# A graph transformer on one core: TensorE's semaphore increments moved from the last product of a group to a drain behind it

## The reference

```python
for l in range(2):
    xn  = layernorm(x)
    xp  = xn + xn @ Wpos + bpos + deg * Wdeg + bdeg      # deg: standardized out-degree
    q, k, v = xp @ Wq + bq, xp @ Wk + bk, xp @ Wv + bv   # 8 heads of 16
    att = clip(sum(q[dst] * k[src]) / 4, -50, 50)
    alpha = softmax of att over the edges of each dst
    x   = x + segment_sum(v[src] * alpha, dst) @ Wo + bo
    x   = x + gelu(layernorm(x) @ W1 + b1) @ W2 + b2     # 128 -> 512 -> 128
out = layernorm(x_in + x)
```

## Time and profile before

| | us |
|---|---|
| median of 3 runs | 3657.33 |
| lowest, highest | 3653.97, 3659.31 |
| span of the profiled execution | 5559.9 |
| TensorE busy in it | 3461.6 (62%) |
| VectorE busy | 2916.7 (52%) |
| GpSimd busy | 2472.4 (44%) |
| ScalarE busy | 1771.1 (32%) |

### The profile page before, as it was taken

How to read it: one execution, slowest core, us unless ns; L and a number is a source line. 1 busy time by engine, 2 the same in 40 slices (tenths; PEclk the granted TensorE clock), 3 DMA queues, 4 the chain that set the end, 5 groups by cost and what they waited for, 6 DMA issues and landing times.

```text
span 5559.9 us, 72300 instructions
## 1 busy us (share of the span) xinstructions
PE 3461.6 (62%) x24196; PEld 2666.6 (48%) x24475; DVE 2916.7 (52%) x6780; ACT 1771.1 (32%) x4391; POOL 2472.4 (44%) x2597
## 2 busy tenths in 40 slices
PE   5834656655665656666566376666666566666666
PEld 4623445444454445444444254455555455545545
DVE  9944545554454545555455354554554454545455
ACT  2301232323333332323234133333333333333334
POOL 1065444444444444444542544445444454444443
PEclk7756777777777777777777677777777777777777
DMA  2133333333333333333332333333333333333332
GB/s 73 49 111 87 88 106 93 102 88 95 102 94 99 94 102 89 104 95 96 107 105 65 106 103 109 108 107 113 96 108 106 108 110 113 111 102 115 109 104 73
DMA packets 404556, 548.28 MB, mean 99 GB/s; under 512 B 78348, under 2 KB 318656, under 8 KB 403988
## 3 DMA queue, kind: packets, MB, share of 16 engines
q0 software_dynamic: 123648, 337.81, 20.9%
q1 hardware_dynamic: 273030, 198.56, 11.9%
q10 hardware_dynamic: 7506, 7.20, 0.4%
HBM read 518.00 MB, written 25.29 MB: 98 GB/s over the span
## 4 chain that ended last, share of the span: by engine, by line
PE 32%; another core or an unknown queue 30%; DVE 14%; issue 12%; ACT 10%; DVEq 0%; SPq 0%; DMA 0%; ACTq 0%
PE psum L952 7%; PE psum L993 4%; PE psum L1009 3%; ACT scratch L1227 3%; PE psum L1042 3%; PE psum L1026 3%; DVE att L1685 2%; PE psum L970 2%; ACT arena L1238 2%; DVE scratch L1676 2%; DVE kv_ring L1394 1%; PE psum L1123 1%; DVE work L1377 1%; DVE scratch L1700 1%
## 5 line engine op out<-in xcount | busy, mean ns | idle before, releaser
L1971 POOL DMA_INDIRECT kv_ring<-kv_table,src_idx x1936 | 1846.4, 954 | 2132.8 <-DVE scratch L1700 1501.1
L1227 ACT ACTIVATE scratch<-psum 128x512 f32<-128x512 f32 x1148 | 649.5, 570 | 2061.3 <-remote 1442.0
L952 PE MATMUL psum<-arena 128*128 128x256 f32 x1764 | 631.5, 486 | 464.2 <-issue 194.2
L1971 POOL DMA_INDIRECT arena<-kv_table,src_idx x640 | 607.8, 950 | 664.6 <-DVE scratch L1700 489.7
L1726 DVE SCALAR_TENSOR_TENSOR arena<-psum,in_block,arena 128x136 f32 x644 | 200.9, 353 | 1286.4 <-remote 1187.3
L993 PE MATMUL psum<-q_win,scratch 64*128 64x128 f32 x5152 | 534.3, 349 | 285.7 <-issue 149.9
L952 PEld LDWEIGHTS psum<-arena 128*128 128x128 f32 x1764 | 372.6, 236 | 621.0 <-issue 319.2
L1009 PE MATMUL psum<-scratch 128*64 128x136 f32 x5152 | 519.1, 330 | 185.4 <-issue 154.2
L993 PEld LDWEIGHTS psum<-q_win,scratch 64*128 64x128 f32 x5152 | 443.2, 243 | 343.1 <-issue 332.5
L1238 ACT COPY arena<-psum 128x512 f32<-128x512 f32 x504 | 265.1, 532 | 986.9 <-remote 524.7
L1685 DVE TENSOR_REDUCE att<-scratch 128x64 f32<-128x1024 f32 (+1 forms) x448 | 525.1, 1172 | 0.1
(11 more groups left out here) (251 smaller groups left out, 4873.9 us busy)
## 6 DMA issues: line engine op xcount, KB each, us to landing
arena<-kv_table SPq DMA_DIRECT2D x126, 896.0 KB
kv_ring<-kv_table,src_idx POOLq DMA_INDIRECT x1936
q_win<-q_table SPq DMA_DIRECT2D x644, 32.0 KB
work<-kv_table SPq DMA_DIRECT2D x98, 128.0 KB
arena<-kv_table,src_idx POOLq DMA_INDIRECT x640
q_win<-q_table SPq DMA_DIRECT2D x126, 64.0 KB
work<-q_table SPq DMA_DIRECT2D x98, 64.0 KB
kv_table<-work SPq DMA_DIRECT2D x49, 128.0 KB
```

Source lines behind the costliest of these rows:

```text
L952: mm = e.matmul(to[:, t % 2 * 2 * D:(t % 2 + 1) * 2 * D], hot_source[:, t * P:(t + 1) * P], source_rows[:, t, :], start=True, stop=True)
L1227: e.activation(to[:, at:at + width], apart[k % 2][:, 0:width], ACT.Relu, bias=1.0, scale=-1.0).then_inc(apart_read, 1)
L1971: e.indirect_dma_start(kv[m % RING_KV][:, t, :], None, kv_table[l], bass.IndirectOffsetOnAxis(ap=src_idx[:, c * T + t:c * T + t + 1], axis ...
```

## The change

In all groups of products of the edge and node stages and of the sorts, the increment is taken off the last matmul, and a drain of TensorE's queue, put behind the group, carries it. In `spread_chunk` one drain increments `spread` by 2. A `sum` of a block has its drain after the second half only. In `node_tensor` one drain stands at the end for all names. The products, their order and the waits stay as they are, as do the first stage and the other engines' programs.

```diff
 source_by_edge:
-            e.matmul(to[:, 0:len(ts) * P], place_source, ..., start=True, stop=True
-                     ).then_inc(apart_made, 1)
+            e.matmul(to[:, 0:len(ts) * P], place_source, ..., start=True, stop=True)
+            e.drain().then_inc(apart_made, 1)
 gather_rows, place_by_edge, edge_by_place: the same, one drain each
 spread_chunk:
-                    m = e.matmul(q_edge[h][:, t * P:(t + 1) * P], ...)
-                    if t == T // 2 - 1:
-                        m.then_inc(spread, 1)
+                    e.matmul(q_edge[h][:, t * P:(t + 1) * P], ...)
+            e.drain().then_inc(spread, 2)
 sum_chunk:
-            m.then_inc(edge_summed, 1)
+            e.drain().then_inc(edge_summed, 1)
 spread_queries:
-            m.then_inc(spread, 1)
+            e.drain().then_inc(spread, 1)
 sum_edges:
             if h == 1:
-                m.then_inc(edge_summed, 1)
+                e.drain().then_inc(edge_summed, 1)
 sort_tensor: in each of totals, slots and rank
-                mm.then_inc(sort_step, 1)
+                e.drain().then_inc(sort_step, 1)
 node_tensor: .then_inc(done, 1) taken off the last product of every name, and at the end
+            e.drain().then_inc(done, 1)
```

More of the change, by code:

```diff
@@ L939, in source_by_edge @@
             to = fill_bank(e, fill(n, "source", h))
-            e.matmul(to[:, 0:len(ts) * P], place_source, edges[:, ts[0] * P:(ts[-1] + 1) * P], start=True, stop=True
-                     ).then_inc(apart_made, 1)
+            e.matmul(to[:, 0:len(ts) * P], place_source, edges[:, ts[0] * P:(ts[-1] + 1) * P], start=True, stop=True)
+            e.drain().then_inc(apart_made, 1)
         def gather_rows(e, n, i):
@@ L951, in gather_rows @@
             for t in range(2 * i, min(2 * i + 2, TB)):
-                mm = e.matmul(to[:, t % 2 * 2 * D:(t % 2 + 1) * 2 * D], hot_source[:, t * P:(t + 1) * P], source_rows[:, t, :],
-                              start=True, stop=True)
-            mm.then_inc(apart_made, 1)
+                e.matmul(to[:, t % 2 * 2 * D:(t % 2 + 1) * 2 * D], hot_source[:, t * P:(t + 1) * P], source_rows[:, t, :],
+                         start=True, stop=True)
+            e.drain().then_inc(apart_made, 1)
         def place_by_edge(e, n, h):
@@ L961, in place_by_edge @@
             to = fill_bank(e, fill(n, "turn", h))
-            e.matmul(to[:, 0:width], of, edges[:, at:at + width], start=True, stop=True).then_inc(apart_made, 1)
+            e.matmul(to[:, 0:width], of, edges[:, at:at + width], start=True, stop=True)
+            e.drain().then_inc(apart_made, 1)
         def edge_by_place(e, n, h):
@@ L969, in edge_by_place @@
             for t in range(0, width, P):
-                m = e.matmul(to[:, t:t + P], edges[:, at + t:at + t + P], of, start=True, stop=True)
-            m.then_inc(apart_made, 1)
+                e.matmul(to[:, t:t + P], edges[:, at + t:at + t + P], of, start=True, stop=True)
+            e.drain().then_inc(apart_made, 1)
         def tensor_fill(e, l, what, u, h):
@@ L1025, in spread_queries @@
             for t in ts:
-                m = e.matmul(q_edge[f % 2][:, (t - ts[0]) * P:(t - ts[0] + 1) * P], hotT[n % 2][:, t * P:(t + 1) * P],
-                             q_win[:, n % 2, :], start=True, stop=True)
-            m.then_inc(spread, 1)
+                e.matmul(q_edge[f % 2][:, (t - ts[0]) * P:(t - ts[0] + 1) * P], hotT[n % 2][:, t * P:(t + 1) * P],
+                         q_win[:, n % 2, :], start=True, stop=True)
+            e.drain().then_inc(spread, 1)
         def sum_edges(e, l, u, h):
@@ L1041, in sum_edges @@
             for t in part_tiles(l, u, h):
-                m = e.matmul(edge_sum(l, u), hot[n % 2][:, t, :], msg[n % 2][:, t, :], start=t == 0, stop=t == last)
+                e.matmul(edge_sum(l, u), hot[n % 2][:, t, :], msg[n % 2][:, t, :], start=t == 0, stop=t == last)
             if h == 1:
-                m.then_inc(edge_summed, 1)
+                e.drain().then_inc(edge_summed, 1)
         def sort_tensor(e, s, k):
@@ L1056, in sort_tensor @@
                 for t in range(ST):
[L1057 to L1059 removed]
+                    e.matmul(ps[0:ST, 0:NT], one_tile[:, ST - 1 - t:2 * ST - 1 - t], s_oh[:, t // RUNS, :, t % RUNS],
+                             start=t == 0, stop=t == ST - 1)
+                e.drain().then_inc(sort_step, 1)
             elif name.startswith("slots"):
@@ L1062, in sort_tensor @@
                 for t in range(RUNS):
-                    mm = e.matmul(ps[0:2 * NT, 0:P], s_vals[:, :, :, t].rearrange("p v b -> p (v b)"), s_slot[:, :, t],
-                                  start=t == 0, stop=t == RUNS - 1)
-                mm.then_inc(sort_placed, 1)
+                    e.matmul(ps[0:2 * NT, 0:P], s_vals[:, :, :, t].rearrange("p v b -> p (v b)"), s_slot[:, :, t],
+                             start=t == 0, stop=t == RUNS - 1)
+                e.drain().then_inc(sort_placed, 1)
             else:
@@ L1070, in sort_tensor @@
                 e.matmul(flat, before[:], s_oh[:, q].rearrange("p b g -> p (b g)"), start=True, stop=False)
-                e.matmul(flat, ones_b[0:ST, :], s_carry[q % 2][0:ST].rearrange("p b g -> p (b g)"), start=False, stop=True
-                         ).then_inc(sort_ranked, 1)
+                e.matmul(flat, ones_b[0:ST, :], s_carry[q % 2][0:ST].rearrange("p b g -> p (b g)"), start=False, stop=True)
+                e.drain().then_inc(sort_ranked, 1)
         def node_tensor(e, l, j, k, held):
@@ L1090, in node_tensor @@
                 if held and j >= LAYERS[l].jb:
-                    mm = e.matmul(ps[:, 0:MW], ident[:], acc_b[:, LAYERS[l].place(j) % HELD_B, :], start=False, stop=True)
+                    e.matmul(ps[:, 0:MW], ident[:], acc_b[:, LAYERS[l].place(j) % HELD_B, :], start=False, stop=True)
                 elif held:
@@ L1095, in node_tensor @@
                         e.matmul(lower, fold[:], acc[:, row, :], start=False, stop=row == ring_rows(2 * j)[-1])
-                    mm = e.matmul(upper, fold[:], acc[:, (2 * j + 1) % RING_W, :], start=False, stop=True)
+                    e.matmul(upper, fold[:], acc[:, (2 * j + 1) % RING_W, :], start=False, stop=True)
                 else:
@@ L1101, in node_tensor @@
                         e.matmul(upper, ident[:, 0:HALF], acc_all[:, 2 * j + 1, :], start=False, stop=False)
-                    mm = e.matmul(ps[:, 0:MW], ident[:], acc_all[:, 2 * j, :], start=False, stop=True)
-                mm.then_inc(done, 1)
+                    e.matmul(ps[:, 0:MW], ident[:], acc_all[:, 2 * j, :], start=False, stop=True)
             elif name == "sums_t":
                 e.wait_ge(mean_ready, nth(l, j, ""))
-                e.transpose(ps[:, 0:P], row, ident[:]).then_inc(done, 1)
+                e.transpose(ps[:, 0:P], row, ident[:])
             elif name == "out_proj":
@@ L1109, in node_tensor @@
                 e.matmul(ps[:, 0:D], ones_b[0:3, :], row_parts[:, l, 0, :], start=True, stop=False)
-                e.matmul(ps[:, 0:D], col, w_o[:, l, :], start=False, stop=True).then_inc(done, 1)
+                e.matmul(ps[:, 0:D], col, w_o[:, l, :], start=False, stop=True)
             elif name == "hidden_t":
                 e.wait_ge(norm_row, norms(l, j, 0))
-                e.transpose(ps[:, 0:P], row, ident[:]).then_inc(done, 1)
+                e.transpose(ps[:, 0:P], row, ident[:])
             elif name == "ff_in":
@@ L1116, in node_tensor @@
                 for i in range(FC):
-                    mm = e.matmul(ps[:, i * P:(i + 1) * P], w_1[:, l, i * P:(i + 1) * P], col, start=True, stop=True)
-                mm.then_inc(done, 1)
+                    e.matmul(ps[:, i * P:(i + 1) * P], w_1[:, l, i * P:(i + 1) * P], col, start=True, stop=True)
             elif name == "ff_out":
@@ L1122, in node_tensor @@
                 for i in range(FC):
-                    mm = e.matmul(ps[:, 0:D], g[:, i * P:(i + 1) * P], w_2[:, l, i, :], start=False, stop=i == FC - 1)
-                mm.then_inc(done, 1)
+                    e.matmul(ps[:, 0:D], g[:, i * P:(i + 1) * P], w_2[:, l, i, :], start=False, stop=i == FC - 1)
             elif name == "next_t":
                 e.wait_ge(norm_row, norms(l, j, 1))
-                e.transpose(ps[:, 0:P], row, ident[:]).then_inc(done, 1)
+                e.transpose(ps[:, 0:P], row, ident[:])
             elif name == "qkv":
                 e.wait_ge(next_ready, i + 1)
-                e.matmul(ps[:, 0:QKV], col, w_qkv[:, l + 1, :], start=True, stop=True).then_inc(done, 1)
+                e.matmul(ps[:, 0:QKV], col, w_qkv[:, l + 1, :], start=True, stop=True)
+            e.drain().then_inc(done, 1)
         def tensor_edges(e):
```

8 lines of the change are left out of this document (4 added, 4 removed).

## The result

The changed kernel takes 4382.27 us (median of 4 runs, 4379.76 to 4383.57), the kernel before 3657.29: ratio 1.199 [1.1973, 1.2007], 725 us slower. Forecast were 4040 us and a range of 3700 to 4500. The direction and the place held; the size was nearly twice the forecast.

A forecast was written before the change was run, and what follows sets the result against it. GpSimd's gathers were taken to bound the kernel at 3657 us; drains would make TensorE the bound, exceeding the gathers by 212 us in layer 0 and 171 in layer 1: 3657 + 212 + 171 = 4040 us, range 3700 to 4500.

The forecast's parts named there:

- The pace before: GpSimd's indirect gathers, 1.25 us apart, set the pace; their sum of 3633.6 us is 0.6% under the median.
- What a drain does: On TensorE's full queue: lost tail overlap (0.16 or 0.07 us), exposed first weight load (0.10 or half), and gap g.
- would have left 3950: If mode switches already drain TensorE, 1288 full/half-array boundaries lose no 0.07 us overlap: 90 us less than 4040.
- TensorE becomes the bound, the ring fills: Main case, 0.78: TensorE exceeds the gathers by 212 and 171 us, the four-chunk ring fills, gathers wait; likeliest 4040 us.
- The increments' lateness is nothing: Increments reach ScalarE and VectorE some 0.1 us later: nothing behind the slot's cover, under 5 us at the layers' ends.
- I take g = 0.12: Gap from products' end to next dispatch behind a drain, two 0.06 us handoffs, range 0 to 0.28; sign: far from 0.12.
- I charge nothing for 1.2: TensorE's clock: the drained queue is as busy, so no time is added for running at 1.2 GHz.
- The products' own time: TensorE's work at full clock without gaps, 1478 and 1481 us in the two layers' counted stretches, partly estimated.
- That is the cover: 400 us per layer: TensorE's undrained 1226 and 1167 us against 1650 and 1570 us of gathers leave 400 us per layer, which drains use up.
- Hidden: Rival, 0.08: the drain passes on dispatch or g is under 0.03, TensorE stays under the gathers; 3657 us, within 5.
- faster: Rival, 0.04: increments on matmuls come slightly late in unrecorded runs too, a drain's do not; at most 24 us gained, 3634.
- All of it counts: Rival, 0.10: TensorE was the bound already, so 354 + 363 us of tails and loads and 444 of gaps add: 4818.

The follow-up runs named there:

- second profile: The kernel before, unchanged, profiled once more: 3644.22 us (8 runs), ratio 0.9992.
- the run with 6 gathers: Changed kernel with 6 gathers per chunk in place of 8 after the first four chunks (output not the reference's): 4335.44 us.
- bare drains: Against the changed kernel, increments back on the last matmul, drains kept behind every group but carrying nothing: 4358.26 us, ratio 1.1951 to the kernel before.
- two drains: Changed kernel with two drains behind each group, the second carrying the increment: 4776.03 us, ratio 1.3088 to the kernel before.
- the chunks' drains: Drains behind the chunks' groups alone (1288), increments on the matmul elsewhere: 3751.72 us; with 6 gathers per chunk 3693.3 us.
- the parts: Changed kernel with drains in some kinds of unit only: chunks 3751.72 us, blocks 3827.93, nodes and sorts 3726.58, chunks with nodes and sorts 3906.16.
- 776 drains: Drains behind the groups of nodes and sorts alone, increments on the matmul elsewhere: 3726.58 us, ratio 1.0223 to the kernel before.
- the bound at 3515 us: The kernel before with 6 gathers per chunk in place of 8 after the first four chunks (output not the reference's): 3514.86 us, ratio 0.9636.
- The same 574 waits: An always met wait ahead of each of 574 hot groups: 4455.08 us in the changed kernel, 3647.42 us (ratio 1.0004) in the kernel before.
- up to 2064 of them: Drains behind the groups of chunks, nodes and sorts, increments on the matmul in blocks: 3906.16 us, ratio 1.0703 to the kernel before.

## Why the prediction was right, and where it was wrong

**The pace before: right, but the sum agreed in part by luck.** The gathers' sum of 3634 us stands against runs of 3644 to 3657. Its start, boundary and end were read from the profile with holes. In the second profile the same sum is 282.8 + 4.9 + 3217.5 + 47.5 + 45.1 = 3598 us, 42 under the span of 3640, and waits between gathers inside the layers (92 - 47 = 45 us) fill the difference. So the gathers set the pace but did wait. To leave the holes out of the sum was right; that recording caused them is not shown.

**What a drain does: right.** Tails no longer overlap, the first load is exposed (the six products of L1042 take 0.96 us behind a drain, and 0.86 without), and a gap follows. What the Trainium skill says of drains (PSUM - Partial Sum Buffer, Engine vs sequencer instructions), that one waits for the engine to be idle, the rows above bear out. Its other rule, that a change of tiling mode drains TensorE (TensorEngine Tiling (Array Packing), Key Properties), would have left 3950. That a chunk's drain costs less than the average (0.14 against 0.22 us) has its sign, but the earlier trace rows show 0.07 us of overlap (by modelled ends) at such a change, which drains take away, and no run separates it.

**TensorE becomes the bound, the ring fills: right.** The waits, the chain and the 47 us of the run with 6 gathers show it. **The increments' lateness is nothing: right**, by the bare drains.

**"I take g = 0.12": wrong, it is 0.20.** The handoff of the earlier trace rows priced a drain with one wait too high (0.08) and missed that almost two thirds of the groups have a wait instruction of their own, which a drained queue no longer hides (0.23). By the prediction's own sign, a gap far from 0.12, this step failed. Gaps of both stretches: 373 + 357 = 730 us, against 444 forecast for the layers and 434 of them here: +296. The 730 hold 60 us of real waits, so the drains' own gaps are nearer 0.19.

**"I charge nothing for 1.2": wrong, some 250 us.** From a mean granted clock of 0.87 and 0.94 between the two levels, TensorE was at 1.2 GHz for a quarter of the first stretch and a ninth of the second (495 and 201 us counted, 423 and 178 of them busy). The same group at each level in the changed kernel:

```profile
910.00 1.15 PE L1009 MATMUL psum<-scratch 128*64 128x136 f32 x16 [0.23 <-issue]
...
1046.06 2.08 PE L1009 MATMUL psum<-scratch 128*64 128x136 f32 x16 [0.23 <-issue]
1048.22 0.50 PE L971 MATMUL psum<-places,arena 128*128 128x128 bf16 x3
```

That is 45% of the slow time in excess, 34% for the hot group (0.59 against 0.39); at 42%, an estimate between them, 601 us hold 253 (204 at 34%, 269 at 45%). The kernel before had 1.2 GHz too (0.92 and 0.93: 16% and 14% of its stretches), but there it cost less: in its 41 runs a mean granted clock lower by 0.01 goes with 9 us more (a straight line through them), while with TensorE the bound it goes with 26 to 31 us more (two drains, 4745.97 us at 0.843 and 4806.63 at 0.820; bare drains, 4350.06 at 0.880 and 4402.49 at 0.863).

**The products' own time: too high by what is left, some 196 us.** Without gaps and at the full clock the stretches hold 1541.6 + 1473.8 - 253 = 2762 us; the working had 1478 + 1481 = 2959. Most of its entries for blocks, nodes and sorts were estimates from column counts.

The three errors sum to 296 + 253 - 196 = 353 us, and the stretches took 3746 against 3393, which is 353. That proves nothing, since the third is the remainder: whatever the clock's part is, from 204 to 269, the products' moves against it. What lies outside them differs by 11 us. So the forecast missed by two terms that point up and one that points down, and without the last it would have been further off: that 4040 came as near as it did is in part luck.

**"That is the cover: 400 us per layer": wrong, and the step to learn from.** It counted TensorE's idle time as free. The idle time was 270 us a layer, and the gathers lie only 134 us in all above the next bound, of which the chunks' drains could use 71. I read it so that TensorE idles while it waits for ScalarE and VectorE, and a drain delays what they wait for; no run tests that. It did not show in the total, since once TensorE is saturated its own work counts and nothing else; it shows in the parts, where 776 drains cost 82 us and "nothing" was expected. "Hidden", at 0.08, and "faster", at 0.04, needed that cover. "All of it counts" had a wrong reason (the gathers do set the pace before) with part of its effect. One sum of the prediction does not follow from its own terms either: at g = 0.04 they give 69 + 24 us too many, 3750 and not 3690, and at 0.03 some 3715, so "hidden" needed a g of practically 0.

What stays open: the bound at 3515 us, what made the holes, and why the clock falls with all 3702 drains and further with two per group, while it stays at 0.89 to 0.90 with up to 2064 of them.

## What to carry to other kernels

Put the increment on the last matmul of a group: then TensorE's queue runs ahead, and here the tail, the next weight load and the waits already met cost nothing; behind a drain each is paid, here 0.2 us for every one of 3702 groups. An engine's idle share is no cover: take the bound away in an experiment and see how far the time falls before adding work beside it. When a recorded span is longer than the runs, profile again before reading its waits.

## What the runs showed of the hardware that was not expected

- Prices on TensorE's queue: end of a group to the next start 0.08 us over a drain, 0.15 more for a wait that is an instruction of its own, though it is met, 0.11 more for another such (0.34 in all), 0.07 more for a second drain. The same 574 waits without drains cost nothing (ratio 1.0004).
- Two profiles of one kernel spanned 5559.9 and 3640.3 us; the first showed increments tens of us late, the second none.
- The mean granted clock was 0.882 to 0.893 without drains, 0.888 to 0.902 with drains in some of the groups, 0.867 to 0.871 with one per group and 0.820 to 0.843 with two, though TensorE was seldom without work for long: most of its gaps with two drains are 0.15 and 0.30 us.
